# A tile loop of 21 steps with a border, and the same loop as one ring of 16 steps per tile

## What is computed

```python
# 1. cross attention of x to a context of 257 rows, 16 heads, latent width 64
h1 = layernorm(x)
q_r = h1 folded with Wq, w_kc_q, W_qr, W_kr           # 16 heads x 64
kv  = rope(ctx)
ctx_c = softmax(q_r @ kv.T) @ kv
x = x + (ctx_c folded with w_kc_kv, Wo)
# 2. self attention within each batch entry (32 tokens), 16 heads of 128, weights codes * scales
h2 = layernorm(x);  q, k, v = h2 @ Wq, Wk, Wv
x = x + softmax(q @ k.T / sqrt(128)) @ v @ Wo
# 3. mixture of experts: 64 experts, top 8 of a softmax router, gate/up 2 x 96, capacity 128
h3 = layernorm(x);  route h3;  x = x + sum of weighted expert outputs
```

## Time and profile before

| | us |
|---|---|
| median of 3 runs | 779.98 |
| lowest, highest | 776.14, 783.31 |
| the profiled execution, its own time | 785.1 |
| its span, first to last instruction | 783.3 |

### The profile page before, as it was taken

How to read it: one execution, slowest core, us unless ns; L and a number is a source line. 1 busy time by engine, 2 the same in 40 slices (tenths; PEclk the granted TensorE clock), 3 DMA queues, 4 the chain that set the end, 5 groups by cost and what they waited for, 6 DMA issues and landing times.

```text
span 783.3 us, 16249 instructions
## 1 busy us (share of the span) xinstructions
PE 622.6 (79%) x6211; PEld 534.6 (68%) x6211; DVE 426.4 (54%) x1091; ACT 288.1 (37%) x798; POOL 294.7 (38%) x279
## 2 busy tenths in 40 slices
PE   6995677898999987898899798898874178898860
PEld 4884566797877876787787696796753067777750
DVE  1255485465676675676576577577653323333334
ACT  1123364337346345236236236246031033333320
POOL 3113299211214414313412412400303337777780
PEclk9975567999999999999999999999999579999995
DMA  7946993999001101100100200100101069999988
GB/s 200 293 140 156 237 251 84 294 338 300 6 2 53 38 3 54 35 3 34 55 3 18 72 2 2 69 2 2 66 2 51 28 167 284 301 301 296 303 168 275
DMA packets 98987, 97.61 MB, mean 125 GB/s; under 512 B 26238, under 2 KB 92848, under 8 KB 98912
## 3 DMA queue, kind: packets, MB, share of 16 engines
q1 hardware_dynamic: 86016, 78.21, 34.2%
q0 software_dynamic: 12288, 17.95, 10.5%
q10 hardware_dynamic: 608, 0.42, 0.2%
HBM read 62.32 MB, written 35.19 MB: 124 GB/s over the span
## 4 chain that ended last, share of the span: by engine, by line
PE 43%; DVE 20%; issue 13%; ACT 9%; POOL 6%; DMA 6%; another core or an unknown queue 2%; SPq 0%; POOLq 0%; DVEq 0%; PEldq 0%; ACTq 0%
POOL expert_sums L545 6%; PE bank L1161 5%; PE bank L1175 5%; PE bank L1142 5%; PE bank L1144 4%; PE bank L1143 4%; PE bank L1207 4%; DMA expert_sums<-Wh,etok 3%; PE bank L1244 3%; ACT pr L609 2%; DVE nmax L830 2%; PE bank L1196 2%; ACT diag L648 2%; ACT space L630 2%
## 5 line engine op out<-in xcount | busy, mean ns | idle before, releaser
L545 POOL DMA_INDIRECT expert_sums<-Wh,etok x64 | 98.8, 1544 | 37.8 <-issue 22.5
L609 ACT ACTIVATE pr<-bank,nmax 128x257 f32<-128x257 f32 x128 | 61.0, 477 | 101.4 <-DVE nmax L830 101.0
L1142 PE MATMUL bank<-space,Wh 128*128 128x128 f16 x512 | 88.3, 219 | 9.9 <-DVE X L928 7.1
L488 POOL DMA_INDIRECT expert_rows<-h,slot x64 | 62.7, 980 | 87.5 <-DVE slot L921 70.4
L1143 PE MATMUL bank<-space,Wh 128*128 128x128 f16 x512 | 88.2, 219 | 0.0
L1144 PE MATMUL bank<-space,Wl 128*128 128x128 f16 x512 | 88.2, 219 | 0.0
L1207 PE MATMUL bank<-Cr,pT 128*128 128x64 f32 x512 | 77.0, 276 | 9.4 <-DVE On L840 8.4
L471 POOL TENSOR_TENSOR Cr<-C,Ct 128x192 f32<-128x192 f32 x64 | 41.7, 675 | 104.9 <-PE bank L1207 104.8
L1207 PEld LDWEIGHTS bank<-Cr,pT 128*128 128x128 f32 x512 | 72.4, 204 | 12.4 <-issue 11.1
L830 DVE TENSOR_REDUCE nmax<-bank 128x1 f32<-128x257 f32 x128 | 53.3, 418 | 42.8 <-PE bank L1189 40.6
L479 POOL TENSOR_TENSOR On<-Cr,pr 128x256 f32<-128x256 f32 x32 | 20.7, 647 | 138.4 <-ACT pr L609 138.4
(11 more groups left out here) (175 smaller groups left out, 1401.0 us busy)
## 6 DMA issues: line engine op xcount, KB each, us to landing
ring<-L_ffn_gate_up_proj_dram SPq DMA_DIRECT2D x64, 192.0 KB
expert_rows<-h SPq DMA_DIRECT2D x8, 1284.0 KB, 15.7
Wh<-expert_rows SPq DMA_DIRECT2D x64, 160.5 KB
ring<-L_ffn_down_proj_dram SPq DMA_DIRECT2D x64, 96.0 KB
expert_sums<-h SPq DMA_DIRECT2D x4, 1152.0 KB, 13.4
C<-ctx_dram SPq DMA_DIRECT2D x24, 128.0 KB, 3.3
Wl<-expert_sums SPq DMA_DIRECT2D x3, 1024.0 KB, 6.9
space<-L_xattn_Wo_dram SPq DMA_DIRECT2D x8, 256.0 KB, 4.8
```

Of the source, the lines that this page charges most:

```text
L488: e.indirect_dma_start(XE[:, :], bass.IndirectOffsetOnAxis(ap=slot[:, k:k + 1], axis=0), h3[:, :], None, bounds_check=E * CAP - 1, oob_is_ ...
L545: e.indirect_dma_start(Y[n % NY][:, :], bass.IndirectOffsetOnAxis(ap=etok[:, n % 4:n % 4 + 1], axis=0), ye[:, n % 4], None, bounds_check=Y ...
L609: e.activation(pr[:, s, :], bank[r % 2][:, 0:NL], ACT.Exp, bias=nmax[:, s:s + 1], accum_out=rsum[:, s:s + 1]).then_inc(expd, 1)
L1142: e.matmul(dst, ah, bh, start=first and n == 0, stop=False)
```

## The change

The loop becomes one ring of 16 steps per tile. Step n of the whole is step t = n mod 16 of group g = n div 16, and there are 16 x 10 + 5 = 165 of them in place of 10 x 21 = 210. Rows run through: the transpose of row n - 2 and the sum of row n - 3 cross into the next tile, whose rows follow at once. So that they can, `hT`, `kt0`, `qa` and `qb` of the next tile move to steps 11, 12, 13 and 15, and `cT3` and `out` of a tile to steps 3 and 4 of the next. Self attention of a tile begins at step 5 (`S_FIRST`) and runs until step 4 of the next group; the routing follows its places. The order of the lists `XS` and the waits follow. The first wait of `sum_row` of a block is now for the first instruction of `normalise` (`x_link`) and not for the last (`on_ready`). On POOL the scatter of tile m stands at step 4, the rope products of the next tile at step 5. The wait for all self attention weights is now reached at step 5 of group 1.

```diff
-XS = ["kt1", "kt2", "cT0", "kt3", "cT1", "cT2", "hT", "qa", "qb", "cT3", "kt0", "out"]
-XNEXT = ("hT", "qa", "qb", "kt0")
-X_AT = {2: ["kt1"], 6: ["kt2"], 7: ["cT0"], 10: ["kt3"], 11: ["cT1"], 15: ["cT2", "hT"], 16: ["qa"], 18: ["qb"],
-        19: ["cT3", "kt0"], 20: ["out"]}
+XS = ["kt1", "cT3", "out", "kt2", "cT0", "kt3", "cT1", "hT", "kt0", "qa", "qb", "cT2"]
+XTILE = {"cT3": -1, "out": -1, "hT": 1, "kt0": 1, "qa": 1, "qb": 1}
+X_AT = {2: ["kt1"], 3: ["cT3"], 4: ["out"], 6: ["kt2"], 7: ["cT0"], 10: ["kt3"], 11: ["cT1", "hT"], 12: ["kt0"],
+        13: ["qa"], 15: ["qb", "cT2"]}
-BEHIND = {0: ["wo0"], 1: ["wo1"], 2: ["wo2"], 3: ["hT", "wo3"], 4: ["q0"], 5: ["q1"], 6: ["q2", "q3"], 7: ["k0", "rT"],
-          8: ["k1", "k2", "log"], 9: ["k3"], 10: ["sc"], 11: ["v0", "pos"], 12: ["v1"], 13: ["v2"], 14: ["v3"],
-          15: ["pv0"], 16: ["pv1"], 17: ["pv2"], 18: ["pv3"]}
+S_FIRST = 5
+S_AT = {5: ["wo0", "wo1"], 6: ["wo2"], 7: ["hT", "wo3"], 8: ["q0", "q1"], 9: ["q2", "q3"], 10: ["k0"],
+        11: ["rT", "k1", "k2"], 12: ["log", "k3"], 13: ["sc"], 14: ["v0"], 15: ["pos", "v1"], 0: ["v2"], 1: ["v3"],
+        2: ["pv0", "pv1"], 3: ["pv2", "pv3"]}
-STEPS = ROWS + 5
+ALL_STEPS = ROWS * (T + 2) + S_FIRST
...
+        def turn_of(g, t):
+            turn = g - 1 if t >= S_FIRST else g - 2
+            j = turn if 0 <= turn < T else None
+            m = turn - 1 if 1 <= turn <= T else None
+            return j, m
...
@@ POOL @@
-            def tile(i, m, last=False):
-                if not last:
-                    rope_products(i + 1)
-                for b in range(BT):
-                    last_rows(i, b)
...
-                    if b == BT - 1 and m is not None:
-                        scatter(m)
-                    if not last:
-                        rope_sums(i + 1, b)
-                if m is not None:
-                    scattered(m)
+            def step(g, t):
+                j, m = turn_of(g, t)
+                if t == 0 and 1 <= g <= T:
+                    last_rows(g - 1, 3)
+                if t == 3 and 1 <= g < T:
+                    rope_sums(g, 3)
+                if t == 4 and g < T:
+                    last_rows(g, 0)
+                if t == 4 and m is not None:
...
+                    scatter(m)
+                if t == 5 and g + 1 < T:
+                    rope_products(g + 1)
+                if t in (7, 11, 15) and g + 1 < T:
+                    rope_sums(g + 1, t // 4 - 1)
+                if t in (8, 12) and g < T:
+                    last_rows(g, t // 4 - 1)
+                if t == 9 and 3 <= g < T + 3:
+                    scattered(g - 3)
@@ DVE @@
+            def step(g, t):
...
+                if g < T:
+                    max_row(g, t)
+                if t % RB == 2 and RB + 2 <= n and n - RB - 2 < T * ROWS:
+                    normalise(*divmod((n - RB - 2) // RB, BT))
...
+                if t == 8 and g + 1 < T:
+                    next_h1(g + 1)
...
+                if j is not None and t == 5:
+                    x_out(j)
+                    norm_root("s", j, mv1, rs1)
+                if j is not None and t == 6:
+                    norm_apply(h2, j, "s", j, mv1, rs1, h2_ready)
...
+                if m is not None and t == 8:
+                    self_out(m)
+                if m is not None and t == 9:
+                    norm_root("r", m, mv2, rs2)
+                if m is not None and t == 10:
...
+                    self_out_norm(m)
...
+                if j is not None and t == 14:
+                    softmax_sum(j)
+                if j is not None and t == 15:
+                    softmax_end(j)
+                if m is not None and t == 13:
+                    chosen(m)
+                if m is not None and t == 0:
+                    weigh(m)
+                if m is not None and t == 1:
+                    place(m)
@@ PE @@
-                if r % RB == 0:
-                    e.wait_ge(on_ready, i * BT + b)
+                if r % RB == 0 and i * BT + b >= 1:
+                    e.wait_ge(x_link, 2 * (i * BT + b) - 1)
```

282 lines of the change are left out of this document (120 added, 162 removed).

## The result

The changed kernel took 829.88 us (825.52 to 831.27, 4 runs), the kernel before in the same series 781.64 us (776.14 to 789.14): a ratio of 1.063, interval 1.055 to 1.071. I had predicted 774 and a range that ended at 790. It is 48 us slower, and no case of mine gave that.

A forecast was written before the change was run, and what follows sets the result against it. PE was taken to set the time, so only its idle time could be won. Start -2.5, turns -0.3, +0.7, +1.5, -3.5, +1.0 and end -3.0 sum to -6.1: 779.98 becomes 774 us, range 757 to 790.

The forecast's parts named there:

- The sum of a turn: Step 5 to step 4, turns 2 to 5: 61.3 becomes 61.7 us each, four turns 246.8 against 245.3, +1.5 us.
- What goes in turns 2 to 5: PE's border wait 3.2, its slow clock 1.7, waits for normalise, norm, self_out and small ones: 10.1 us a turn saved.
- What comes: Six new PE waits a turn in turns 2 to 5, the largest 3.2 us in step 15: 9.6 us together.
- The norm beside the product: DVE's step 6: norm h2 is stretched beside POOL's rope products, 2.4 us charged ahead of hT.
- Rival (b): DVE reaches norm h2 before the rope product and POOL waits: 2.4 us less in turns 2 to 5, 764 us; chance 0.2.
- The clock: Step 15's wait may bring back TensorE's slow clock; half of its 1.7 us a turn was taken.
- rival (c): Step 15's wait lowers the clock every turn and qb runs at half rate: 3.6 us a turn, 790 us; chance 0.18.
- Turns 0, 1 and 6: Turn 0 54.6 against 54.9 us, turn 1 58.1 against 57.4, turn 6 48.5 against 52.0.
- Turn 7: Up to its last pv: chosen stands ahead of the softmax sum, 39.1 becomes 40.1 us, +1.0.
- The start: Self attention of the first tile begins at 142.4 us against 144.9: -2.5 us.
- The end: DVE takes up the last wo sooner, as the last scatter ends before it: -3.0 us, with 0 and -3.5 as ends.
- Rival (a): New waits mostly hidden as DVE and ACT run ahead: 4.9 us a turn gained over turns 1 to 6, 748 us; chance 0.12.

The follow-up runs named there:

- e12: The kernel before, with POOL sending one row in place of 128 for each of a tile's eight scatters: 758.16 us, ratio 0.968.
- e2: The changed kernel with DVE's shift of the self attention scores ahead of qa's parts and chosen moved to step 14: 813.90 us, ratio 1.077.
- both moves: The changed kernel with POOL's rope products ahead of the scatters, the scores' shift ahead of qa's parts and chosen in step 14: 791.55 us, ratio 1.049.
- e3: The changed kernel with 122 matmuls without use a turn in seven of PE's waiting places: 799.62 us, ratio 1.060.
- e10: The changed kernel with products first, DVE reordered and pv0 in step 2, plus 56 matmuls without use a turn, against the same without them: 809.09 us, ratio 1.041.

## Why the prediction was wrong

**The sum of a turn.** I had 61.3 - 10.1 + 9.6 + 0.85 = 61.7 us; 68.1 were measured (272.5 / 4). Of the 6.4 that are missing, 2.1 are idle time of PE (+1.2 foreseen, +3.3 measured) and 4.3 are its clock (-0.85 foreseen, +3.5 measured).

**"What goes in turns 2 to 5 ... Together 10.1."** This is the step that failed. I booked the border's 3.2 us and its 1.7 of slow clock as waits of the ring's chain that vanish with the border. The border's wait did vanish, but most of its price wasn't the border's. With the scatters cut (e12) all four borders of these tiles wait 1.58 us ahead of `kt0` and none ahead of `out`, and `out` takes 3.62 us:

```profile
410.23 2.00 PE L1160 MATMUL bank<-h1T,M 128*128 128x128 f32 x16
412.27 1.18 ACT L587 CAST qspace<-bank 64x512 f16<-64x512 f32 x2 [1.65 <-PE bank L1160]
413.47 1.39 DVE L823 TENSOR_TENSOR qspace<-bank,qspace 64x512 f16<-64x512 f32 x2 [0.97 <-ACT qspace L587]
414.92 0.55 PE L1165 MATMUL bank<-ident,Cr 128*128 128x128 f32 x3 [1.58 <-DVE qspace L823]
```

Here ACT takes up `qb` 0.04 us behind its end, and not 0.95. So of my 4.9 us some 1.6 were the border's and 3.3 came with the scatters, which the ring keeps. I priced the wait by its last releaser and didn't ask why the releaser was late. Cut out of the kernel before, the scatters give 3.9 us a turn (61.3 to 57.4), out of the ring 6.5 (68.1 to 61.7), as far as traces of different series can be compared. The ring puts them in steps 4 to 7, where `out`, its norm and `hT` form a chain of DVE instructions with little beside it, and DVE starts a maximum there 1.5 to 3.9 us late once a turn. My price for moving the scatters was POOL's time alone. That the ring without scatters takes the 61.7 us that I had foreseen is luck: it stands against 57.4 and not 61.3.

**"What comes", 9.6 us.** The waits were read rightly: step 15 at 3.0 (predicted 3.2), `v2` at 0.8 (0.9), and row 0's transpose with `pv0` at 2.3, more than now at the upper end of 0 to 2.5. The norm beside the product was the right mechanism in another place: the product met `normalise` (L835, 1.45 us), and with it `cT0`, as well as the norm. The two together cost 4.9 us a turn with their clock on a chip without stops (e2 against both moves), where I had 2.4. Rival (b), that they miss each other, came about only when I moved the products.

**The clock.** I took half of 1.7 us a turn; rival (c) took 3.6. Measured are 13.9 us in four turns, 3.5 a turn above what the kernel before already pays; without the scatters it is 1.9 a turn (7.5 in four). The waits are not much longer than the ones they replaced, but there are six or more of them, and the mean clock fell to 0.92; in the first series, where it was 0.95 to 0.97, matmuls in the waits brought it to 1.00 (e3). That (c) was nearest to this, and that I gave it 0.18, was the second error: I summed the waits one by one and gave each its own length as its price.

**Turns 0, 1 and 6** failed by the same causes: 63.8 and 57.4 in two traces (predicted 54.6), 62.6 and 63.4 (58.1), 54.8 and 55.0 (48.5). **Turn 7** came near the number, 38.8 and 39.9 for 40.1, but in part by luck: up to its last `pv` the kernel before takes 37.5 and not the 39.1 of the earlier trace rows, which end 1.5 us behind it. **The start** didn't gain: self attention begins at 147.7 and 143.1 in the two traces of the changed kernel and at 145.6 and 147.4 in those of the kernel before. With its scatters cut, which come only later, the kernel before begins it at 136.9, and all traces here lie between that and 154.4, so one trace could not have told 2.5 us. **The end** did: from the last `pv` to the take-up of `wo` it is 7.0 us and not 10.6, 3.6 won for my 3.0. In the kernel before it was a late start too: L928 starts 3.75 us behind the last `wo`, the last scatter being under way, and with the scatters cut (e12) 0.04 us behind it.

Rival (a) has a slip: 29 us off 774 are 745, not 748.

My range came from the bounds of the waits that I had listed; no bound covered an effect that the moved transfers have on engines which don't wait for them.

## What to carry to other kernels

When a wait's releaser is late, follow the chain back on the timeline to an instruction whose last input had ended well before it started. The labels "issue" and "remote" alone don't show one: DVE's 1.9 us of "issue" were a wait for ACT, and the late one was ACT, whose label named PE. If such a late start is found, the time belongs to something else that was going on, here a row of indirect DMAs, and goes where that goes. Price a move of DMAs by what runs beside them in the new place. And count new waits, not only their sum: in four turns 13.3 us more of waiting cost 13.9 us of clock, and matmuls without use in the waits (17 us won in e10) are a cheap test of how much. Compare only kernels of one chip and one series; two of my readings were the chip's.
